# Windowed attention in a fused network: probabilities transposed in 32x32 squares on VectorE, values as the stationary operand

## What is computed

```
qkv = x @ Wqkv                       # x: 4 x 512 x 128 after a token shift; 16 heads of 64
q, k = l2norm(q) * qs, l2norm(k) * ks
q, k = rotary(q), rotary(k)
sim  = q_window @ k_window.T * 8     # 32 queries see the 32 keys before and their own 32
p    = softmax(where(mask, sim, -big))
out  = (p @ v_window) @ Wo ;  x = x + out
x    = x + (a * gelu(gate)) @ W2     # a, gate = halves of layernorm(x') @ W1
```

## Time and profile before

| | |
|---|---|
| time, median of 3 runs (lowest, highest) | 2197.83 us (2191.8, 2197.89) |
| span of the profiled execution, first to last instruction | 2182.5 us |
| mean granted TensorE clock | 0.985 of full speed |
| PE busy | 2005.7 us (92%) |
| DVE busy | 1809.4 us (83%) |
| ACT busy | 1579.9 us (72%) |
| POOL busy | 1167.3 us (53%) |
| transfers | 132.18 MB, mean 61 GB/s |

### The profile page before, as it was taken

One profiled execution on the slowest core, in us unless ns is written; L12 is line 12 of the kernel. 1 busy time (PEld: TensorE's weight loads), 2 busy tenths in 40 slices (PEclk: granted clock), 3 DMA queues, 4 the chain that ended last, 5 costly groups with the idle time before them and its releaser, 6 DMA issues.

```text
span 2182.5 us, 82607 instructions
## 1 busy us (share of the span) xinstructions
PE 2005.7 (92%) x34395; PEld 1457.7 (67%) x34395; DVE 1809.4 (83%) x3751; ACT 1579.9 (72%) x3031; POOL 1167.3 (53%) x1413
## 2 busy tenths in 40 slices
PE   6888899987699999999999999999999999999997
PEld 4666654455577776777777777777767777677775
DVE  7888765678798998888988888988888988888884
ACT  4777753365577887787877788777787878887773
POOL 1112110000577676666776667666667767667761
PEclk9999999998899999999999999999999999999999
DMA  4000001000122232222322223322232322332221
GB/s 114 1 2 2 2 31 59 30 1 30 52 72 68 61 105 69 68 63 71 90 72 75 66 58 95 81 68 66 70 87 71 87 58 58 102 82 62 75 59 40
DMA packets 98196, 132.18 MB, mean 61 GB/s; under 512 B 27900, under 2 KB 42882, under 8 KB 97826
## 3 DMA queue, kind: packets, MB, share of 16 engines
q1 hardware_dynamic: 97826, 126.90, 22.0%
HBM read 28.20 MB, written 1.11 MB: 13 GB/s over the span
## 4 chain that ended last, share of the span: by engine, by line
PE 72%; DVE 13%; issue 6%; ACT 6%; POOL 1%; SPq 1%; DMA 0%; DVEq 0%; POOLq 0%; ACTq 0%
PE oo L586 21%; PE pj L586 19%; PE tr L589 14%; PE sc L586 13%; ACT arena L1924 3%; PE tr L586 2%; DVE arena L1729 2%; DVE xn L1318 2%; DVE arena L1486 1%; PE oo L589 1%; DVE arena L1731 1%; DVE arena L1750 1%; DVE arena L1752 1%; PE sc L589 1%; ACT sc L1924 1%
## 5 line engine op out<-in xcount | busy, mean ns | idle before, releaser
L2345 POOL TENSOR_TENSOR arena<-arena 128x1024 f32<-128x1024 f32 x192 | 456.9, 2380 | 336.9 <-DVE arena L1731 336.9
L1924 ACT ACTIVATE arena<-tr 128x512 f32<-128x512 f32 (+2 forms) x874 | 460.8, 570 | 111.9 <-PE tr L589 109.7
L1924 ACT ACTIVATE arena<-pj 128x512 f32<-128x512 f32 x576 | 341.7, 599 | 189.5 <-PE pj L586 150.4
L589 PE MATMUL tr<-ident,arena 128*128 128x128 f32 x2882 | 413.3, 279 | 25.3 <-DMA beta<-in_L_attn_betas 9.8
L1924 ACT ACTIVATE arena<-arena 128x16 f32<-128x16 f32 (+6 forms) x808 | 362.3, 454 | 98.7 <-DVE arena L1486 74.0
L589 PEld LDWEIGHTS tr<-ident,arena 128*128 128x128 f32 x2882 | 330.6, 141 | 93.4 <-issue 34.5
L2363 POOL TENSOR_TENSOR arena<-arena 128x1024 f32<-128x1024 f32 x192 | 366.7, 1910 | 23.2 <-POOL arena L2356 0.9
L1729 DVE TENSOR_TENSOR arena<-pj,rtab 128x512 f32<-128x512 f32 x384 | 259.8, 677 | 24.8 <-ACT arena L1924 23.4
L586 PE MATMUL oo<-slab,arena 64*32 64x64 f32 (+1 forms) x12416 | 232.1, 228 | 41.0 <-issue 26.4
L1731 DVE TENSOR_TENSOR arena<-pj,rtab 128x512 f32<-128x512 f32 x384 | 261.4, 681 | 0.0
L1737 DVE TENSOR_REDUCE arena<-arena 128x8 f32<-128x512 f32 x384 | 255.6, 677 | 0.0
(11 more groups left out here) (289 smaller groups left out, 3802.5 us busy)
## 6 DMA issues: line engine op xcount, KB each, us to landing
slab<-arena SPq DMA_DIRECT2D x576, 128.0 KB, 2.4
slab<-arena SPq DMA_DIRECT2D x336, 64.0 KB, 2.0
wqkv<-in_L_ffn_Wqkv SPq DMA_DIRECT2D x18, 512.0 KB, 4.2
arena<-gate_mem SPq DMA_DIRECT2D x24, 256.0 KB, 4.3
wo<-in_L_ffn_Wo SPq DMA_DIRECT2D x6, 512.0 KB, 4.2
w<-in_L_ffn_W SPq DMA_DIRECT2D x6, 341.0 KB
YT<-in_L_attn_x SPq DMA_DIRECT2D x4, 256.0 KB, 3.5
arena<-in_L_ffn_W SPq DMA_DIRECT2D x1, 1024.0 KB
```

The lines of the kernel that those rows point to most:

```text
L589: return nc.tensor.transpose(o, i, ident[0:i.shape[0], 0:i.shape[0]])
L1924: return nc.scalar.activation(o, i, f, **k)
L2345: p_.tensor_tensor(r_, r_, rb[:, k, :], ALU.add).then_inc(sum_ok, 1)
```

## The change

**Softmax and values.** POOL now multiplies the exponents by the inverse sums in place (`normalise`), so `weighted` is gone. DVE turns all 16 heads' probabilities of the tile in one transpose instruction over 128 x 1024 elements, in squares of 32 x 32 (`turn_probs`), from SBUF to SBUF; the 8 transposes on TensorE and ACT's two copies (`take_probs`) are gone. `values` has 128 calls in place of 64: for each head, window and half of the keys one call with the values (32 keys by 64 columns) as stationary operand and the turned probabilities (32 columns) as moving operand. Two calls add up in PSUM, the former window's keys and the own ones. The result comes out turned, so `turn_out` is gone. The four windows write four banks (two of `oo`, two of `tr`). They stand in one run of 128 calls, and `window_scores` in one run of 64.

**Pipeline.** The values of tile g-3 are weighed in slot g, behind P0 and P1 (before: g-2, in two halves around the turning of the keys). P4 and P5 now stand behind the scores with P0 and P1 of the next slot right behind them. The feed-forward chunks move to t = 1 (chunk 0) and t = 3 (chunks 1 and 2), all in `oo`, with the Gelu table loaded ahead of them by an instruction of its own (`gelu_tables`). `ff_down` of batch n-3 stands in t = 1, `norm_back` in t = 0.

**The rest.** `lengths` sums the squares of a whole query or key row (two instructions of 1024 elements a tile in place of four of 512). The layer norm reads a copy in SBUF (`turned_rows`). `windows` has 1 or 2 transfers a tile. The copy of the layer's columns (`lcur`) is gone.

```diff
-            def lengths(g, c):
-                k, hf = c // 2, c % 2
-                v.tensor_reduce(ss[:, k, hf * PAIRS:(hf + 1) * PAIRS, 0],
-                                sq[:, c % 2].rearrange("p (h d) -> p h d", d=DL), AX.X, ALU.add
+            def lengths(g, k):
+                v.tensor_reduce(ss[:, k, :, 0], sq.rearrange("p c (h d) -> p (c h) d", d=DL), AX.X, ALU.add
                                 ).then_inc(ss_ok, 1)
...
+            def turn_probs(g):
+                ve.wait_ge(en_ok, g + 1)
+                wait(ve, o_mm, g)
+                v.transpose(PT.rearrange("p h j q -> p (h j q)"), Ex.rearrange("p h k -> p (h k)")
+                            ).then_inc(pt_ok, 1)
...
+            def normalise(g):
+                gp.wait_ge(ri_ok, g + 1)
+                p_.tensor_tensor(Ex, Ex, ri.unsqueeze(2).broadcast_to([P, HL, 2 * WIN]), ALU.mult
+                                 ).then_inc(en_ok, 1)
...
+            def values(g):
+                n, t = divmod(g, T)
+                pe.wait_ge(pt_ok, g + 1)
...
+                for pr in range(PAIRS):
+                    for j in range(2):
+                        for u in range(2):
+                            f = slice((2 * pr + u) * DL, (2 * pr + u + 1) * DL)
+                            for w in range(G):
+                                k_ = slice(w * WIN, (w + 1) * WIN)
+                                v_ = Vt[k_, t, f] if j else Vp[k_, t % 2, f]
+                                last = mm(VBANK[w][u * DL:(u + 1) * DL, pr * WIN:(pr + 1) * WIN], v_,
+                                          PT[k_, 2 * pr + u, j, :], start=(j == 0), stop=(j == 1),
+                                          skip_group_check=True)
+                last.then_inc(o_mm, 1)
```

More of the change, by code:

```diff
@@ L402, in __init__ @@
                 self.g = self.n * T + t
[L403 to L413, removed]
+                self.later = l > 0
+                self.m1 = self.n - 1 if self.n >= 1 else None
+                self.m2 = self.n - 2 if self.n >= 2 else None
+                self.m3 = self.n - 3 if self.n >= 3 else None
+                self.y0, self.y1, self.y2, self.y3 = ((b - k) % B * S for k in range(4))
+                self.ahead = None if b == B - 1 and l == DEPTH - 1 else (b + 1) % B * S
         def run_slots(slot):
@@ L1063, in ff_up, with wo_half, ff_down @@
                 mm(bank[0:w, 1], w1[:, o:o + w], hB).then_inc(w1_mm, 1)
+            def wo_half(m, i):
+                half = slice(i * (S // 2), (i + 1) * (S // 2))
+                for p_ in range(PAIRS):
+                    last = mm(oo[:, i, half], wo[:, p_, :], oT[:, p_, half], start=(p_ == 0),
+                              stop=(p_ == PAIRS - 1))
+                last.then_inc(wo_mm, 1)
+            def ff_down(m, bank):
+                for k, (o, w) in enumerate(CH):
+                    pe.wait_ge(ff_ev, m * FFC + k + 1)
+                    last = mm(bank, w2[0:w, k, :], fa[0:w, k, :], start=(k == 0), stop=(k == FFC - 1))
+                last.then_inc(w2_mm, 1)
@@ L1135, in ff_down @@
-                def ff_down(m):
-                    pe.wait_ge(ff_ev, m * FFC + 3)
-                    for k, (o, w) in enumerate(CH):
-                        last = mm(oo[:, 0], w2[0:w, k, :], fa[0:w, k, :], start=(k == 0), stop=(k == FFC - 1))
-                    last.then_inc(w2_mm, 1)
-                if new:
-                    if b == 0 and t == 0:
-                        pe.wait_ge(wl_ok[0], l + 1)
-                    queries(0)
-                    queries(1)
-                    if g > 0:
-                        crossing(g, 1)
@@ L2202, in slot @@
+                ac.wait_ge(ss_ok, g * 2 + 1)
+                square(g, 2)
+                if g == 0:
+                    crossing(g, 1)
                 if layer_end:
                     table(g + 1, l + 1, 0)
-                if d_:
-                    take_probs(g2, 0)
-                if s_.ahead is not None and t == 1:
+                square(g, 3)
+                if t == 3 and m2 is not None:
+                    gelu_tables()
+                else:
+                    inverse_root(g, 0)
@@ L2207, in slot @@
+                if g >= 1:
+                    take_qk_part(g - 1, (t - 1) % T, 0)
+                    take_qk_part(g - 1, (t - 1) % T, 1)
+                    mask(g - 1, (t - 1) % T)
+                if t == 0:
+                    wait(ac, pj_mm, n * (6 * T))
+                    shifted(xs_hi, YT[:, s_.y0:s_.y0 + S], P, S).then_inc(xs_h, 1)
+                if s_.ahead is not None and t == 2:
                     if l > 0 or b == B - 1:
```

750 lines of the change are left out of this document (306 added, 444 removed).

## The result

The changed kernel takes 2650.5 us (median; 2621.9 to 2659.1) where the kernel before takes 2195.8 on the same chip: a ratio of 1.204, 95% interval 1.198 to 1.211. The forecast was 2400 with a range of 2210 to 2480. The direction was right; the size was missed by 250 us, more than half of the whole loss of 455. The profiled execution spans 2657.2 us, 474.7 more than before.

A forecast was written before the change was run, and what follows sets the result against it. PE, busy 92%, was taken as the bound. Slots summed to 74.25 us a batch against 66.0: 2182.5 + 198 (24 batches) + 3 (drain) = 2383.5, plus 15.3, about 2400 us; range 2210 to 2480.

The forecast's parts named there:

- Block stops: In the run of 256 value pairs: PE uses up a 256-instruction block in 1.34 us, next after 3.4, standing 2.06.
- The price of a chunk: Projections on PE: a chunk of three split matmuls of 512 columns taken at 0.7 us.
- rival 3: Whole kernel faster: TensorE's work decides, standing and ACT waits hide; about 2080 to 2130 us; chance 0.12.
- the forecast's own 74.25: Sum of the four slots on PE, us a batch, against 66.0 before: +8.25, in 24 batches +198.
- The values' pace: Run of 256 value pairs on PE: 10.5 ns a pair, 2.7 us, plus 0.2 for start and emptying.
- rival 1: In the values run: loads set the pace, 24.4 ns a pair, run 6.2 us, about 2563 us; chance 0.08.
- the estimate of 25 ns a pair: Value pairs: the skill page's 60 cycles a matmul would make the run 6.4 us, where the forecast has 2.7.
- Waits for ACT: PE waiting for ACT's copies at scores and first chunks: 9.05 us a batch, t = 3 the longest slot.
- Rival 2: Only one of two effects, standing for instruction blocks or waits for ACT, is there: 2200 to 2300 us; chance 0.18.
- The transposes: 16 of 32 a tile leave PE, -1.7 us; DVE's new transpose of 1024 elements 1.22, at most twice that.

The follow-up runs named there:

- both edits: Changed kernel with values in pieces between projection chunks, and chunks 4, 5 and ACT's work in another order: 2380.0 us, ratio 1.088 to the kernel before.

## Why the prediction was wrong in size and right in direction

The step that failed is the price of the work in the slots. The sum took every step at the full clock and put what stops of 2 us do to the work behind them at nothing, and it took a chunk at the price of a dense row. The runs showed 8 to 9 us a batch for the first and 3.4 for the second. The idle time that the prediction is mainly about came out as forecast.

- **Block stops, right.** Forecast one of 2.06 a run. Every one of the 94 runs from 650 to 2650 us has the stop behind the block that lies wholly in it, 1.93 in the mean. To it come 0.34 a run, against the sentence "the blocks on both sides of it reach into projections and last long enough": in 24 of the 94 runs, each with 80 or more pairs ahead of the first boundary, PE stops there as well, as in the rows above. Together that is 8.9 a batch in the runs, and 0.5 elsewhere.
- **The clock, missing.** No step of the working asked what stops of 2 us do, though each number before them was taken from rows at a clock of 1.00. Comparing the same steps with before: projections 24.0 against 20.2, transposes 9.6 against half of 14.4, feed-forward 8.4 against 7.1, output projection 7.2 against 6.7. That is 8.0 a batch, 192 us, three quarters of the error. The changed kernel's own rows bear it out: a chunk that runs wholly at the full clock takes 0.84 us, the same as before, at the low clock 1.38. Priced by its own steps at the full clock, its steps at the low one cost 9.2 a batch more, of which 1.7 lie in the values; so the 1.0 that the sum below gives to the values is clock as well.
- **The price of a chunk, too small.** "a chunk of three: 0.7" is the pace inside dense rows. From a chunk's start to the start of the next step it is 0.84 in the mean in the kernel before, 0.70 for one that stands behind another chunk and 0.89 to 0.91 for one that stands alone between steps of another shape: 3.4 a batch. The prediction had the sign of this in hand. Its rival 3 says that PE's work of today comes to 60 by its prices and takes 66; of these 6, 2.9 are work and 3.2 idle time. It used that ratio for the rival and compared the forecast's own 74.25, at bare prices, with the measured 66.0.
- **The values' pace, right.** 10.5 ns a pair and ends of 0.2 were 2.94 a run; measured 3.2, and 2.8 at the full clock. The source was a row of another form, so some luck is in it. The even pace of 24 ns (rival 1) is excluded by the 98 pairs from 1734.06 on, 10 ns each. Excluded too is the estimate of 25 ns a pair from the Trainium skill, "TensorEngine Tiling (Array Packing)", section "Instruction Overhead", as a floor. Its advice against splitting a dimension that is small already agrees with these runs for another reason: each pair is two instructions of a block, and with half the pairs the changed kernel takes 350 us less.
- **Waits for ACT, right.** 9.05 forecast, 7.0 measured, at the two places named (scores and first chunks), and the t = 3 slot is the longest, 23.8 us against 19.4 to 21.8 for the others. Rival 2, that one of the two effects isn't there, fell, and so did rival 3: with 65.2 to 68.8 of work there is no 57 on PE to be bound by.
- **The transposes.** -1.7 us a tile on PE is right (14.4 a batch before; 7.7 with both edits, at a clock of 0.97), DVE's transpose is 1.235 us, the lower end of 1.22 to 2.4, and neither it nor POOL is waited for in the changed kernel.
- **The sum.** 10.9 a batch were missing: the clock 8.0, chunks 3.4, stops 1.2, values 1.0, other steps -0.7, ACT -2.0.

## What to carry to other kernels

Count instructions, not only time: where small matmuls used up 256 instructions in less than the 3.4 to 3.7 us measured here, the engine stood for the rest, and spreading the same pairs between long matmuls brought 184 us, though each chunk between them then took 0.1 us longer. Before pricing new idle time on TensorE, ask what the clock does behind it, and add a term for the work that follows. Price the kernel before by the same bare steps as the new one, and carry the difference to its measured time into the forecast.

## What the runs showed that was not expected

- Idle stretches of 1.75 to 2.25 us behind small pairs were mostly followed by some 3 to 7 us at 1.2 GHz (44 of 60); those behind large matmuls mostly weren't (11 of 46).
- A block of 256 instructions took 3.47 to 4.02 us with almost no other transfers beside it (9% DMA share with the pairs doubled), no less than the 3.4 to 3.7 worked out from the kernel before at 28%. So fewer transfers didn't make it quicker here.
- Removing a wait can make a kernel slower: 13 us of waits for the norm's step became 38 us more of idle time ahead of the values, which by the order of ACT's rows are waits for ACT.
- "issue" isn't always a lack of instructions. Where it stands ahead of a run that has a wait in front, it can be that wait.
